# A two-layer decoder on one core: the second batch's choice moves into the cross attention, and the last stage turns the next batch's tokens before its second products

## The reference, cut to what matters

```python
def _L1_ffn_ref(x, w_r, b_r, W1, b1, W2, b2):      # x: (4, 1024, 256)
    k = int(CAPACITY * s)                          # CAPACITY = 0.5, s = 1024: k is 512
    weights = (jnp.einsum('bsd,do->bso', x, w_r) + b_r).squeeze(-1)
    top_vals, _ = jax.lax.top_k(weights, k)
    threshold = top_vals[:, -1]
    selected = weights > threshold[:, None]
    hidden = jax.nn.gelu(jnp.einsum('bsd,dh->bsh', x, W1) + b1, approximate=False)   # W1: 256 x 1024
    blk = jnp.einsum('bsh,hd->bsd', hidden, W2) + b2                                 # W2: 1024 x 256
    return jnp.where(selected[..., None], blk, x)
...
x = _layernorm(x + _L1_xattn_ref(x, ctx, ...))     # the stage c1 of the kernel
x = _layernorm(x + _L1_ffn_ref(x, ...))            # the last stage of the kernel
```

## Time and profile before

| | us |
|---|---|
| median of 3 runs | 3369.74 (3367.74 to 3370.96) |
| the profiled execution | 3372.37 |
| its span, first to last instruction | 3370.3 |
| PE busy | 2874.1 (85%) |
| DVE busy | 1620.1 (48%) |
| ACT busy | 1134.7 (34%) |
| POOL busy | 1690.0 (50%) |

### The profile page before, as it was taken

How to read it: one execution, slowest core, us unless ns; L and a number is a source line. 1 busy time by engine, 2 the same in 40 slices (tenths; PEclk the granted TensorE clock), 3 DMA queues, 4 the chain that set the end, 5 groups by cost and what they waited for, 6 DMA issues and landing times. The chain is left out here.

```text
span 3370.3 us, 41933 instructions
## 1 busy us (share of the span) xinstructions
PE 2874.1 (85%) x11729; PEld 1690.7 (50%) x11729; DVE 1620.1 (48%) x3330; ACT 1134.7 (34%) x1613; POOL 1690.0 (50%) x1430
## 2 busy tenths in 40 slices
PE   7999999999999999999999688828993788688755
PEld 5555555555555555555555344317883344333333
DVE  4555555555555545555555346621114345357632
ACT  2333333333333333333333235411112222245223
POOL 2665666666666666666666612246665122222332
PEclk8999999999999999999999889968996778799778
DMA  4322332232233323222332110036763000000232
GB/s 123 73 65 62 73 75 70 67 75 64 59 73 75 71 65 75 67 58 71 75 73 69 51 52 2 2 113 217 225 221 102 7 0 0 26 2 8 37 105 78
DMA packets 152384, 238.13 MB, mean 71 GB/s; under 512 B 31430, under 2 KB 76526, under 8 KB 152302
## 3 DMA queue, kind: packets, MB, share of 16 engines
q1 hardware_dynamic: 127486, 166.97, 19.8%
q0 software_dynamic: 20864, 64.06, 6.5%
q10 hardware_dynamic: 3952, 6.08, 0.5%
HBM read 89.68 MB, written 29.38 MB: 35 GB/s over the span
## 5 line engine op out<-in xcount | busy, mean ns | idle before, releaser
L601 POOL TENSOR_TENSOR a_total<-a_total,a_pr 128x1024 f32<-128x1024 f32 x384 | 908.5, 2366 | 264.3 <-ACT a_pr L585 250.7
L541 DVE TENSOR_REDUCE a_nmax<-a_psX 128x1 f32<-128x512 f32 x1024 | 672.8, 681 | 365.2 <-PE a_psX L536 355.2
L585 ACT ACTIVATE a_pr<-a_psS 128x1024 f32<-128x1024 f32 x512 | 522.3, 1024 | 814.2 <-PE a_psS L576 769.7
L536 PE MATMUL a_psX<-a_kA,a_qA 128*128 128x512 f32 x1024 | 469.7, 485 | 40.7 <-DVE a_nmax L541 19.3
L613 PE MATMUL a_psO<-a_pr,a_vd 128*64 128x512 f32 x2048 | 481.8, 602 | 0.0
L576 PE MATMUL a_psS<-a_qA,a_kA 128*128 128x512 f32 x1024 | 340.1, 413 | 0.2 <-ACT a_pr L585 0.2
L576 PE MATMUL a_psS<-a_qB,a_kB 128*128 128x512 f32 x1024 | 320.3, 394 | 1.1 <-DVE a_qB L558 1.1
L536 PEld LDWEIGHTS a_psX<-a_kA,a_qA 128*128 128x128 f32 x1024 | 183.4, 189 | 252.1 <-DVE a_nmax L541 116.8
L601 POOL TENSOR_TENSOR a_total<-a_pr 128x1024 f32<-128x1024 f32 x64 | 152.8, 2387 | 300.6 <-ACT a_pr L585 300.6
L613 PEld LDWEIGHTS a_psO<-a_pr,a_vd 128*64 128x64 f32 x2048 | 129.9, 136 | 246.1 <-issue 224.3
L576 PEld LDWEIGHTS a_psS<-a_qA,a_kA 128*128 128x128 f32 x1024 | 188.2, 189 | 81.6 <-issue 50.5
(11 more groups left out here) (345 smaller groups left out, 3984.4 us busy)
## 6 DMA issues: line engine op xcount, KB each, us to landing
a_qA<-a_qhi SPq DMA_DIRECT2D x256, 128.0 KB, 2.3
a_kA<-a_khi SPq DMA_DIRECT2D x128, 128.0 KB, 2.3
a_kA<-a_klo SPq DMA_DIRECT2D x128, 128.0 KB, 2.3
a_kB<-a_khi SPq DMA_DIRECT2D x128, 128.0 KB, 2.3
a_qB<-a_qlo SPq DMA_DIRECT2D x128, 128.0 KB, 2.3
a_vd<-a_vg SPq DMA_DIRECT2D x128, 128.0 KB
sorted_in<-g_zero SPq DMA_DIRECT2D x4, 1280.0 KB
e_xg<-sorted_in SPq DMA_DIRECT2D x40, 128.0 KB
```

The source lines that it names most:

```text
L536: w.eng.matmul(psX[:, half, :], qA[:, b, u * P:(u + 1) * P], kA[:, b, half * 512:(half + 1) * 512], start=True, stop=True).then_inc(sems[" ...
L541: w.eng.tensor_reduce(nmax[:, half, u:u + 1], psX[:, half, :], AX.X, ALU.max, negate=True)\
L585: w.eng.activation(pr[:, n, :], psS[:, half, :, :].rearrange("p a b -> p (a b)"), ACT.Exp, scale=SCALE)\
L601: w.eng.tensor_tensor(total[:, buf, :], first, pr[:, n, :], ALU.add).then_inc(sems["ad"], 1)
```

## The change

In the second cross attention the slots are filled otherwise. `weigh(1, c)` moves from the slots (6,3) to (7,2) into block 5, beside the counts of batch 0, with `write(1)` and `read(1)` behind it. The eight counts of batch 1 stand in (6,3) and block 7, `weigh(2, c)` and `write(2)` in block 7 too, and `choose(1)` in its last slot. After the last block come `rank(1)` and `hall.load(0)`, and behind the last layer norm the first two scatters of batch 1. `xc` has become a tile of `hall`, so that it can be loaded ahead of the last stage. In its place `W2` (1 MB) and `b2` are loaded at the start of the last stage and no longer three stages earlier.

In the last stage PE does `turn(b+1)` ahead of all of `down(b)`, with `rank(2)` between them, and `rank(3)` inside `up(1)`. ACT does `turn(b+1)` ahead of all eight picks of batch b-1, and of the two halves of the layer norm the second is put off until after the second gelu of the next batch. DVE begins with weighing batch 3 and counting batch 2.

```diff
@@ choice_step
+            if n == 5:
+                hall.weigh(w, 1, c)
+                if c == 3:
+                    hall.write(w, 1)
+            if (n, c) == (6, 0):
+                hall.read(w, 1)
...
-                rank_first(w)
-            if 11 <= 4 * (n - 4) + c <= 14:
-                hall.weigh(w, 1, 4 * (n - 4) + c - 11)
+                rank(w, 0)
+            if (n, c) == (6, 3):
+                hall.count(w, 1, 0)
             if n == 7:
                 hall.scatter(w, 0, 2 * c)
                 hall.scatter(w, 0, 2 * c + 1)
-                if c == 2:
-                    hall.write(w, 1)
+                hall.count(w, 1, 2 * c + 1)
+                if c < 3:
+                    hall.count(w, 1, 2 * c + 2)
+                hall.weigh(w, 2, c)
                 if c == 3:
-                    hall.read(w, 1)
+                    hall.write(w, 2)
+                    hall.choose(w, 1)
@@ walk, behind the last block
+            if hall is not None:
+                rank(w, 1)
+                hall.load(w, 0)
             for half in range(2):
                 outputs(w, NB - 1, half)
             for half in range(2):
                 normed(w, NB - 1, half)
+            if hall is not None:
+                for t in range(2):
+                    hall.scatter(w, 1, t)
@@ chosen_mlp, sync
-            load(w, 0)
-            hall.write(w, 2)
+            eng.dma_start(w2[:, :, :], hall.W2.rearrange("(a p) c -> p a c", p=P)).then_inc(sems["w"], 16)
+            eng.dma_start(b2s[:, :], hall.b2.partition_broadcast(P)).then_inc(sems["w"], 16)
             hall.read(w, 2)
+            load(w, 1)
             hall.write(w, 3)
             hall.read(w, 3)
-            load(w, 1)
@@ chosen_mlp, gpsimd
+            for t in range(2, TB):
+                hall.scatter(w, 1, t)
...
-            for b in range(1, 3):
-                for t in range(TB):
-                    hall.scatter(w, b, t)
+            for t in range(TB):
+                hall.scatter(w, 2, t)
@@ chosen_mlp, vector
+            for k in range(TB // 2):
+                hall.weigh(w, 3, k)
             for t in range(TB):
-                hall.count(w, 1, t)
-            hall.choose(w, 1)
...
             hall.choose(w, 2)
             rank(w, 2)
+            for i in range(CT):
+                down(w, 0, i)
+                hall.count(w, 3, 2 * i)
+                hall.count(w, 3, 2 * i + 1)
             hall.choose(w, 3)
+            rank(w, 3)
...
-                if b == 1:
-                    rank(w, 3)
-                shift(w, b - 1, 0)
                 add(w, b - 1, 1, 0)
+                shift(w, b - 1, 0)
@@ chosen_mlp, scalar
                     up(w, b, hc)
-                if b:
-                    for t in range(GR):
-                        pick(w, b - 1, t)
+                    if b > 1 and hc == 1:
+                        normed(w, b - 2, 1)
                 if b + 1 < B:
                     turn(w, b + 1)
                 if b:
-                    for t in range(GR, TB):
+                    for t in range(TB):
                         pick(w, b - 1, t)
                     normed(w, b - 1, 0)
-                    normed(w, b - 1, 1)
+            normed(w, B - 2, 1)
@@ chosen_mlp, tensor
-                    if b == 0 and hc == 5:
-                        rank(w, 1)
-                    if b == 1 and hc == 3:
-                        rank(w, 2)
-                down(w, b, 0)
-                down(w, b, 1)
-                if b == 1:
-                    rank(w, 3)
-                down(w, b, 2)
+                    if b == 1 and hc == 1:
+                        rank(w, 3)
                 if b + 1 < B:
                     turn(w, b + 1)
-                down(w, b, 3)
+                if b == 0:
+                    rank(w, 2)
+                for i in range(CT):
+                    down(w, b, i)
```

More of the change, by code:

```diff
@@ L165, in __init__ @@
         names = ["cst", "wr", "w", "pr", "wd", "col", "cnt", "selb", "sel", "pd", "at", "bk"]
-        names += [f"{n}{b}" for n in ("out", "rows", "sc") for b in range(B)]
+        names += [f"{n}{b}" for n in ("out", "rows", "sc", "x") for b in range(B)]
         self.s = {n: self.sem(n) for n in names}
@@ L282, in scatter, with load @@
                 .then_inc(self.s[f"sc{b}"], 16)
+    def load(self, w, b):
+        if w.on("sync"):
+            w.eng.wait_ge(self.s[f"sc{b}"], 16 * self.TB)
+            w.eng.dma_start(self.xc[:, b % 2, :, :], self.apart[b][0:self.KEEP, :].rearrange("(t p) c -> p t c", p=P))\
+                .then_inc(self.s[f"x{b}"], 16)
 def make_identity(pool, tile, sem):
@@ L1125, in normed, with rank @@
             w.inc("y", 2)
-        def rank_first(w):
+        def rank(w, b):
             k = bank(w)
@@ L1130, in rank_first @@
                 w.wait(f"m{k}", w.at(f"m{k}"))
-                hall.rank(w, 0, psM[:, k, :]).then_inc(sems["mi"], 1)
+                hall.rank(w, b, psM[:, k, :]).then_inc(sems["mi"], 1)
             w.inc("mi")
@@ L1136, in rank_first @@
                 w.wait(f"m{k}", w.at(f"m{k}", -1))
-                hall.places(w, 0)
+                hall.places(w, b)
             w.inc(f"m{k}")
@@ L1629, in load @@
             if w.on("sync"):
-                w.eng.wait_ge(hall.s[f"sc{b}"], 16 * TB)
                 w.wait("tr", b - 1)
-                w.eng.dma_start(xc[:, b % 2, :, :], hall.apart[b][0:KEEP, :].rearrange("(t p) c -> p t c", p=P))\
-                    .then_inc(sems[f"x{b}"], 16)
+                hall.load(w, b)
         def turn(w, b):
             if w.on("tensor"):
-                w.wait(f"x{b}", 16)
+                w.eng.wait_ge(hall.s[f"x{b}"], 16)
                 w.wait("xt", 2 * b)
@@ L1640, in turn @@
                     for t in range(CT):
-                        last = w.eng.transpose(psT[:, cc, t * P:(t + 1) * P], xc[:, b % 2, t, cc * P:(cc + 1) * P], ident[:, :])
+                        last = w.eng.transpose(psT[:, cc, t * P:(t + 1) * P], hall.xc[:, b % 2, t, cc * P:(cc + 1) * P], ident[:, :])
                 last.then_inc(sems["tr"], 1)
@@ L1659, in up @@
             if w.on("scalar"):
[L1660 removed]
+                w.eng.wait_ge(hall.s["w"], 32)
                 w.wait("h", n + 1)
@@ L1667, in down @@
             if w.on("tensor"):
+                w.wait("w", 32)
                 w.wait("he", (b + 1) * HC)
@@ L1674, in down @@
             if w.on("vector"):
-                w.eng.wait_ge(hall.s["w"], 64)
+                w.wait("w", 32)
                 w.wait("o", n + 1)
@@ L1764, in _ @@
             load(w, 2)
-            down(w, 1, 0)
-            down(w, 1, 1)
-            normed(w, 0, 0)
-            down(w, 1, 2)
-            down(w, 1, 3)
-            normed(w, 0, 1)
-            load(w, 3)
-            for b in range(2, B):
+            for b in range(1, B):
                 down(w, b, 0)
@@ L1777, in _ @@
                 down(w, b, 3)
+                if b == 1:
+                    load(w, 3)
                 normed(w, b - 1, 1)
@@ L1847, in _ @@
                 down(w, b, 1)
-                if b == 1:
-                    rank(w, 3)
+                add(w, b - 1, 1, 0)
                 shift(w, b - 1, 0)
-                add(w, b - 1, 1, 0)
                 down(w, b, 2)
```

51 lines of the change are left out of this document (12 added, 39 removed).

## The result

The changed kernel takes 3334.88 us, median of four runs (3330.49 to 3336.22), beside 3369.53 for the kernel before on the same chip: ratio 0.9895, 95% interval 0.9878 to 0.9912. Faster, and inside the forecast's range. The profiled execution took 3335.51, its span is 3333.4; before they were 3372.37 and 3370.3. The span is 36.9 us shorter: the cross attention took 12.7 us more, the last stage 49.6 less up to TensorE's (PE's) last product, and the tail stayed at 29.6.

What follows compares the result with a forecast made beforehand. PE was taken to set the cross attention's pace, and the last stage to be a chain of waits for `xc` and gelus. Cross attention +12.1 and last stage -50.7 gave -38.6 us: 3333.8 profiled, 3331 median, range 3322 to 3344.

Steps and rivals of the forecast that it cites:

- Which waits bound the last stage: Last stage: PE's stalls of 18.5 us for batch 1's load and 12.1 for a gelu go, last product 50.7 us sooner.
- The turn ahead of the second products: Last stage, PE: batch 1's turn takes 1.04 us, of which 0.84 fills the wait for the last gelu.
- Masks behind the copies, norm halves apart: Last stage, ACT: the half layer norm within the first products of batches 2 and 3 may hold PE 0.5 us each.
- Block 5: Cross attention: one weighing more per slot on DVE, partly hidden in its waits, costs 2.4 us, bounds 0 and 5.9.
- Block 7: Cross attention: added DVE counts and weighing stand ahead of PE's next product in every slot, 9.3 us, bounds 5 and 12.5.
- The end: End of the cross attention: POOL's two scatters, 2.5 us, plus the way to the barrier, against 2.97 of slack: 0.4 us more.
- Rival A: Last stage: PE waits at the turn of batch 1 or the rank of batch 2, price 3 to 8 us; chance 0.09.
- Rival B: Last stage: late POOL gathers hold ACT's norm ahead of batch 2's first products, up to 12.1 us paid; chance 0.09.
- C: Cross attention pays everything, 19 us instead of 12, because DVE's delay also cools PE's clock: 3338 us; chance 0.07.
- D: Last stage: batch 2's rank holds PE for long, each us of late row costing one, slower than before; chance 0.02.
- E: The change doesn't act: transposes come earlier in the order but the stalls only change place; chance 0.03.
- From trace to median: Whole kernel: the profiled execution stood 2.6 us above its median, so the forecast of 3333.8 becomes 3331.

Runs made afterwards that it cites:

- the second trace: The changed kernel run again without any edit, on the chip of the follow-up runs: 3307.88 us, ratio 0.9900 to the kernel before.
- The run with the choice alone: The changed kernel with PE's turns late and ACT's order in the last stage as before, the early choice kept: ratio 0.9920 to the kernel before.
- The pairings: Changed kernel with PE's turn and ACT's order each new or old; ratios: both new 0.9900, only turn new 0.9893, only ACT new 0.9919, both old 0.9920.
- the two weighings taken out: The changed kernel without the end scatters, two of batch 2's four weighings moved from block 7 into the last stage: ratio 0.9918 to the kernel before.
- the run with the row first: The changed kernel with the read of batch 2's row ahead of W2 and b2 on SP's queue: ratio 0.9913 to the kernel before.
- the run of the order alone: The kernel before with the last stage's new orders of PE, ACT, DVE and SP, batch 1's choice left in the last stage: ratio 0.9993.
- the run without the end scatters: The changed kernel with batch 1's first two scatters moved from the cross attention's end to the last stage's start: ratio 0.9894 to the kernel before.

## Why the forecast was right, step by step

- *Which waits bound the last stage*: right. Both stalls are gone; T0 to last product went from 176.1 to 126.5, forecast 125.4. PE's busy time in this stretch fell by 9.1 us (129.3 to 120.2) at a higher granted clock, 0.96 for 0.85; that is part of what the forecast called the rest. The gaps of 2.5 and the rank's 0.66 made it longer than laid out, the 1.0 that I had put in for the norms did not show; without the gaps, in the second trace, it is 122.7.
- *The turn ahead of the second products*: right in direction, but I priced only what it fills (0.84 us a batch) and gave the 12.1 us to a norm that comes sooner. The run with the choice alone shows that the early choice by itself takes 9 of the 12.1. The pairings show that with the early choice and the turn late, 12 to 14 us of trace remain, in ACT's or DVE's queue by ACT's order. The sum still came out, since both sides of the cut were in the change.
- *Masks behind the copies, norm halves apart*: I gave them no term but a cost of 1 us. With the early turn they are worth 0.2 us of trace, and with a late turn nothing either (135.44 with ACT's new order, 133.70 with the old one).
- *Block 5*: forecast +2.4, measured +2.7 (0.6 in its window, 2.1 in the next).
- *Block 7*: forecast +9.3 (its four terms add up to 9.2). DVE's last operation ends 42.5 us into it, not 34.8: +7.7. The DVE terms were right, +9.0 up to the last transposition; what the sum left out is the shorter projection behind it, 5.18 for 6.51. Why it is shorter no run separates. That DVE's work there is paid one for one is shown by the two weighings taken out: 2.8 us of work, 3.1 us of path.
- *The end*: forecast +0.4, measured +2.2. The failing step is the bound that I took for the way to the next stage: I used ACT's 0.87, but behind POOL's last scatter the way is 2.75 long. Without the scatters 2.2 us go. Together block 7 and the end are +10.0 for +9.7, and the cross attention +12.7 for +12.1: that this sum came out so well is luck, an error of -1.6 against one of +1.8. The sign "DVE without idle time in 7" did not come: it still waits 2.71 and 2.29 us for output projections.
- *Rival A*, a wait at `turn(1)` or `rank(2)`: did not occur. The choice of batch 2 was made at T0'+18.9, PE came at +21.6. The doubt about W2 ahead of the row was half right: by the run with the row first it put DVE's first count 2.1 us later, and the margin held. The reason for taking no delay failed: the issues of W2 and b2 took 0.37 and 0.58 us, not 1.7 and 3.7, so SP was not held back. In return the row was used 7.2 us after its issue, not 3.9 to 6.1, and the first count came at T0'+8.7, where 9.3 to 11.5 were laid out. Two errors cancelled. The rule that I took from the Trainium skill, "DMA: Bandwidth & Descriptors", section "Issuing engines are not separate DMA queues", agrees with the runs: the load of batch 1 took 7.6 us with the row 1.2 us ahead of it and 3.9 in the changed kernel, and POOL's scatters landed later beside SP's 4 KB write, 9.8 us for 6.6 at the slowest.
- *Rival B*, ACT's stall stays: did not occur. *C*, cross attention pays all of it, clock included: not in the first trace, in part in the others. From block 5's start to the last stage it is 93.0 us in the run of the order alone and 105.4 to 108.4 in the six later traces with the changed cross attention: 12.4 to 15.4 more (12.4 and 13.9 in the two on the same chip), and a lower clock stands beside it (last section). *D* occurred only in an experiment. *E* did not.
- *From trace to median*: the forecast took the profiled execution 2.6 us above its median; the one after stood 0.6 above, so the medians differ by 34.7, not 36.9.

## What to carry to other kernels

An order change that lets an engine run ahead pays when its inputs are there, and inputs that come early pay when nothing queued in front holds them: here the order alone gave nothing measurable, the choice alone about four fifths of the gain by the ratios. The place of W2 has no run of its own. Before moving a small DMA by one slot, list everything that is queued behind it, on its own issuing engine: a 4 KB write 0.4 and 0.6 us in front of the wrong transfer made PE wait 9.0 us in one run and 9.2 in another. And read each length from two executions before explaining the last 3 us of it.

## What the runs showed of the hardware

TensorE's clock after a short wait is not the same from one execution to the next. At the end of block 5 the change makes PE wait for DVE ahead of an output projection; the wait is 3.08 to 3.10 us in ten traces. The projection takes 1.99 us in the first of them and 2.71 to 3.78 in the nine others. In the first trace of the changed kernel, and in the second:

```profile
3110.16 1.99 PE L1090 MATMUL c_psM<-c_wo,c_oT 128*128 128x256 f32 x8 [3.08 <-DVE c_oT L1063]
```

```profile
3080.84 3.40 PE L1090 MATMUL c_psM<-c_wo,c_oT 128*128 128x256 f32 x8 [3.08 <-DVE c_oT L1063]
```

The window from block 6 to 7 of three kernels with the same cross attention up to there: the changed kernel's second trace, the run with the row first, and the run without the end scatters:

```profile
3072.00:3099.99 27.99, 22.20 (x117) 9.93 (x115) 23.97 (x60) 11.53 (x13) 6.87 (x13) 0.94 0.08 21
```

```profile
3072.72:3102.45 29.73, 24.44 (x117) 11.51 (x115) 24.17 (x60) 11.43 (x13) 6.89 (x13) 0.83 0.08 20
```

```profile
3074.71:3104.44 29.73, 24.44 (x117) 11.51 (x115) 24.18 (x60) 11.43 (x12) 6.89 (x13) 0.83 0.07 20
```

The granted clock of the window goes from 1.00 (26.59 us) over 0.94 to 0.83 with the length, at the same instructions. The kernel with the choice as before had 0.93 and 25.45 us on one of these chips, against 1.00 and 24.47 in its first trace, so part of it comes without the change. Why the clock falls in one execution and not in another after the same wait stays open, as does what the gaps of 2.5 us in the first trace were; the kernel before has gaps of 2.33 and 1.62 us in the same products of the program.

A small write holds up what is issued right behind it on SyncE, in all three places of these traces where that occurs. Four transfers of 8 KB, 0.4 us behind a 4 KB write that took 10.0 us, were used 10.3 us after their issue. A row of 512 KB, 0.6 us behind one that took 11.2, landed after 11.1, where the same row took 4.4 in the run whose queue has it ahead of that write. And in the changed kernel itself the load of batch 0 stands 0.65 us behind the write of batch 2's weights at the end of the cross attention: it landed after 12.7 us, after 12.8 in the second trace and 12.3 without the end scatters, and after 3.7 and 3.8 in the two runs in which that write had moved away. There it is hidden under the layer norm. No trace tells why.
